# Row and edge jobs moved into the counting stage, and x and node numbers side by side in one gathered table, in a graph kernel on one Trainium2 core

## What is computed

```python
h = relu(edge_attr @ W1.T + b1); w = h @ W2.T + b2          # edge jobs
agg = segment_sum(w * x[src], dst, N)
x = layernorm(x + relu(x @ Ws.T + bs + agg @ Wn.T + bn))    # row jobs where agg = 0
# then: 10 passes of out = 0.9 * spmm(out) + 0.1 * h, a layernorm,
# 16 passes of h = 0.9 * A_norm(h) + 0.1 * x, a layernorm,
# two graph convolutions with PReLU, a layernorm
```

## Time and profile before

| | us |
|---|---|
| median of 3 runs | 12,517.22 (12,501.07 to 12,523.01) |
| the profiled execution | 12,463.33 |
| its span in the profile | 12,461.6 |
| busy in the span: PE, DVE, ACT, POOL | 4,407; 4,689; 3,793; 7,373 |
| first 2,681 us: all that stands ahead of the passes | 21.5% of the span |
| granted TensorE clock, mean | 0.548 of full |

### The profile page before, as it was taken

One profiled execution on the slowest core, in us unless ns is written; L12 is line 12 of the kernel. 1 busy time (PEld: TensorE's weight loads), 2 busy tenths in 40 slices (PEclk: granted clock), 3 DMA queues, 4 the chain that ended last, 5 costly groups with the idle time before them and its releaser, 6 DMA issues. The chain is left out here.

```text
span 12461.6 us, 88179 instructions
## 1 busy us (share of the span) xinstructions
PE 4407.2 (35%) x18774; PEld 3275.0 (26%) x18774; DVE 4688.8 (38%) x11607; ACT 3793.3 (30%) x11417; POOL 7372.8 (59%) x7464
## 2 busy tenths in 40 slices
PE   4610462343333333332033333333334332212533
PEld 3300352332222222221022222222222221111422
DVE  7900232233333333355034444444444443233333
ACT  3400462243222222226342222222223231134322
POOL 6767105426666667665656666666666666654455
PEclk8655555555555555555555555555555555555555
DMA  3211221133333333333123333333333333221211
GB/s 51 56 26 20 67 83 44 38 71 88 85 88 88 85 88 90 87 84 104 34 79 87 88 89 88 88 93 94 95 94 98 95 96 82 73 57 54 63 35 31
DMA packets 791320, 919.85 MB, mean 74 GB/s; under 512 B 258979, under 2 KB 676541, under 8 KB 790749
## 3 DMA queue, kind: packets, MB, share of 16 engines
q1 hardware_dynamic: 558638, 591.29, 15.5%
q0 software_dynamic: 232064, 323.36, 13.4%
q10 hardware_dynamic: 144, 0.10, 0.0%
HBM read 533.07 MB, written 388.06 MB: 74 GB/s over the span
## 5 line engine op out<-in xcount | busy, mean ns | idle before, releaser
L1624 POOL DMA_INDIRECT l_g<-tab,l x4704 | 4620.1, 982 | 2536.7 <-issue 1355.4
L1824 DVE TENSOR_TENSOR_SCAN l_w<-l_m,l_w,bank 96x512 f32<-96x512 bf16 x1248 | 1590.3, 1274 | 4350.1 <-remote 2797.1
L1661 PE MATMUL bank<-ident,l_w 96*128 96x96 f32 x5096 | 1092.0, 364 | 2537.9 <-DVE l_w L1824 2176.1
L1724 ACT ACTIVATE l_o<-l_o,coef_d 128x96 f32<-128x96 f32 x2940 | 857.1, 363 | 3162.2 <-DVE l_o L1852 1813.6
L1650 PE MATMUL bank<-ident,l_g 128*96 128x128 f32 x5096 | 1267.5, 399 | 1345.3 <-DMA l_g<-tab,l 602.5
L1661 PEld LDWEIGHTS bank<-ident,l_w 96*128 96x128 f32 x5096 | 846.5, 222 | 2833.4 <-DVE l_w L1824 2368.4
L1650 PEld LDWEIGHTS bank<-ident,l_g 128*96 128x96 f32 x5096 | 913.4, 190 | 1725.1 <-DMA l_g<-tab,l 640.4
L1720 ACT ACTIVATE l_o<-bank,coef_s 128x96 f32<-128x96 f32 x1764 | 450.4, 345 | 1809.7 <-remote 970.6
L278 PE MATMUL bank<-tail_up,v 96*96 96x500 f32 (+1 forms) x298 | 296.4, 1098 | 925.7 <-issue 660.4
L993 POOL DMA_INDIRECT XS<-in_x_dram,dst_i x196 | 198.0, 1010 | 710.7 <-DVEq L1337 647.3
L315 PE MATMUL bank<-ident,tail_up 96*125 96x96 f32 (+1 forms) x596 | 159.5, 423 | 867.8 <-issue 476.2
(11 more groups left out here) (292 smaller groups left out, 10764.1 us busy)
## 6 DMA issues: line engine op xcount, KB each, us to landing
tab<-l_o SPq DMA_DIRECT2D x1176, 192.0 KB
l_g<-tab,l POOLq DMA_INDIRECT x4704
l_m<-mask_d SPq DMA_DIRECT2D x784, 96.0 KB
l_m<-mask_s SPq DMA_DIRECT2D x490, 96.0 KB
x3t<-XS SPq DMA_DIRECT2D x98, 192.0 KB
prep_x<-in_x_dram SPq DMA_DIRECT2D x100, 187.5 KB
x1t<-prep_a SPq DMA_DIRECT2D x100, 187.5 KB
x3d<-prep_b SPq DMA_DIRECT2D x100, 187.5 KB
```

The source lines that it names most:

```text
L1624: nc.gpsimd.indirect_dma_start(out=tile(G[q % RG], t), out_offset=None, in_=tables[0:table_at + (2 - p % 2) * TR, :] if p else first, in_o ...
L1661: last = nc.tensor.transpose(b_bank(q)[:, u * D:(u + 1) * D], W[q % RW][:, u:GE:U], self.ident[0:D, 0:D])
L1724: last = a.activation(tile(O[q % RO], t), tile(O[q % RO], t), ACT.Copy, scale=self.coef_d[:, t:t + 1])
L1824: v.tensor_tensor_scan(out=W[q % RW][:, :], data0=masks[q % RM][:, :], data1=a_bank(q)[0:D, :], initial=W[(q - 1) % RW][:, GE - 1:GE] if q ...
```

## The change

Row jobs and edge jobs leave `prepare` and run inside `count_edges`, which is now written out for every engine: iteration k does tiles 2k and 2k+1, row job k (its steps spread over the following four iterations) and every other time an edge job. Row and edge jobs get one PSUM bank for each step (4 to 7) instead of two; x buffers are 8 instead of 5, result buffers 4 instead of 3; they, the count tables and the edge attributes lie in a new tile XM [128, 196 x 104]. XS is no longer allocated this early. SP also copies x into a new table `x_meta` of 104 floats a node, in 25 pieces, between its other transfers.

In `prepare`, SP copies `meta` beside x in that table. POOL gathers `meta` by source, waits for the copy, and gathers x and `meta` together by destination: two rounds instead of three. Edge records are made in two halves: the first (groups 0 to 24) ahead of the sums loop as soon as its rows have landed, the second ahead of the loop's group 12 (FIRST); the scatter waits for each half by itself. In the sums loop one semaphore ("stepped") stands for several, and its steps lag by one more turn. The core of the diff:

```diff
+HALF, FIRST = 25, 12
+        self.both_t = self.dram("x_meta", [N, D + MF])
+            self.XM = tmp("XM", [P, NT * (D + MF)])
...
             @block.sync
+                for k in range(LAST):
+                    n = k // 2
+                    if k % 2 == 0 and n < NI - 1:
+                        if n:
+                            sp.wait_ge(nears, n * U)
+                        load(n + 1)
+                    if k + 3 < JN:
+                        load_x(k + 3)
+                    if k % 4 == 1 and k // 4 < JOIN:
+                        some = slice(k // 4 * (N // JOIN), (k // 4 + 1) * (N // JOIN))
+                        sp.dma_start(self.both_t[some, 0:D], i["x"][some, :]).then_inc(R["joined"], 16)
+                    if 0 <= k - 5 < JN:
+                        store_rows(k - 5)
...
             @block.vector
+                for k in range(LAST):
+                    for t in (2 * k, 2 * k + 1):
+                        if t < NT:
+                            pairs(t)
+                            if t + 1 < NT:
+                                digits(t + 1)
+                        if 0 <= t - 2 < NT:
+                            tiles_before(t - 2)
+                        if t % U == 2 and t // U + 1 < NI:
+                            high_digits(t // U + 1)
+                        if t % 2 == 0:
+                            if 0 <= k - 2 < JN:
+                                rows(k - 2)
+                        else:
+                            if 0 <= k - 3 < JN:
+                                scale_rows(k - 3)
+                            if k % 2 and 0 <= (k - 3) // 2 < NI:
+                                gate((k - 3) // 2)
...
             @block.tensor
+                    for t in (2 * k, 2 * k + 1):
+                        if t < NT:
+                            count(t)
+                        if 0 <= t - 1 < NT:
+                            lookup(t - 1)
+                        if t % U == 0 and 0 <= n - 1 < NI:
+                            weigh(n - 1)
+                        if t % U == 1 and n < NI:
+                            if n == 0:
+                                pe.wait_ge(R["ea"], 32)
+                            turn_edges(n)
+                        if t % U == 3 and n < NI:
+                            hide(n)
+                        if t % 2 == 0:
+                            if k < JN:
+                                turn_rows(k)
+                        elif 0 <= k - 1 < JN:
+                            mult_rows(k - 1)
...
             @block.scalar
+                    for t in (2 * k, 2 * k + 1):
+                        if t < NT:
+                            snapshot(t)
+                        if t % U == 0 and 0 <= n - 1 < NI:
+                            rectify(n - 1)
+                        if t % U == 2 and n < NI:
+                            copy_edges(n)
+                        if t % 2 == 0:
+                            if 0 <= k - 4 < JN:
+                                normal_rows(k - 4, 0)
+                        else:
+                            if k < JN:
+                                lift_rows(k)
+                            if 0 <= k - 2 < JN:
+                                root_rows(k - 2)
+                            if 0 <= k - 4 < JN:
+                                normal_rows(k - 4, 1)
...
     def prepare(self):
+                for k, (index, of, into) in enumerate(((self.src_i, self.meta, ms), (self.dst_i, self.both_t, rows_in))):
+                    if k:
+                        pool.wait_ge(S["joined"], 16)
+                    for g in range(NGP):
+                        q = k * NGP + g
                         if q >= RG:
                             pool.wait_ge(self.fills(q), self.full(q - RG))
...
                 for g in range(NGP):
-                    q = 3 * NGP + g
+                    q = 2 * NGP + g
+                    if g in (0, HALF):
+                        pool.wait_ge(S["made"], 1 + g // HALF)
...
             @block.sync
+                    sp.dma_start(self.both_t[:, D:D + MF], self.meta[0:N, :]).then_inc(S["joined"], 16)
...
             @block.vector
+                for g in range(NGP + 3):
+                    if g in (0, FIRST):
+                        part = g // FIRST
+                        landed = NGP + (NGP if part else HALF)
+                        for q in range(landed - RG, landed):
+                            dve.wait_ge(self.fills(q), self.full(q))
+                        self.edge_records(dve, link, halves[part], part, ms, md, work[part], record, row, S)
+                        dve.sem_inc(S["made"], 1)
                     if g < NGP:
                         scan(g)
```

More of the change, by code:

```diff
@@ new lines, in _ @@
+                load(0)
+                for n in range(3):
+                    load_x(n)
+                sp.wait_ge(R["blank"], 1)
+                with nc.allow_non_contiguous_dma(reason="the attributes of four edges of each partition"):
+                    sp.dma_start(ea[:, 0:GF * U * ED].rearrange("p (g c) -> p g c", c=U * ED),
+                                 i["ea"][0:GF * GE, :].rearrange("(g p u) c -> p g (u c)", p=P, u=U)
+                                 ).then_inc(R["ea"], 16)
+                    sp.dma_start(ea[0:REST // U, GF * U * ED:NT * ED],
+                                 i["ea"][GF * GE:E, :].rearrange("(p u) c -> p (u c)", u=U)).then_inc(R["ea"], 16)
@@ new lines, in turn_edges, with hide, weigh @@
+                    last.then_inc(G["turned"], 1)
+                def hide(n):
+                    pe.wait_ge(G["copied"], n + 1)
+                    nc.tensor.matmul(edge_in[0:D, :], self.w1[:, :], eat[:, :], start=True, stop=True
+                                     ).then_inc(G["hidden"], 1)
+                def weigh(n):
+                    pe.wait_ge(G["rect"], n + 1)
+                    if n:
+                        pe.wait_ge(G["gated"], n)
+                    for u in range(U):
+                        last = nc.tensor.matmul(edge_out[:, u * D:(u + 1) * D], hid[:, u * P:(u + 1) * P], self.w2[:, :],
+                                                start=True, stop=True)
+                    last.then_inc(G["product"], 1)
@@ L808, in lookup @@
-                def lookup(t, u, b):
-                    pe.wait_ge(split.sem, split.at + t + 1)
-                    if not (isinstance(t, int) and t < 2):
-                        pe.wait_ge(fars.sem, fars.at + t - 1)
-                    k = 0
-                    for c in range(2):
-                        for part in (coarse, fine):
-                            last = nc.tensor.matmul(look[u % 2], oht[:, b, c, u * P:(u + 1) * P],
-                                                    part[u % 2][:, c * LO:(c + 1) * LO], start=k == 0, stop=k == 3)
-                            k += 1
-                    last.then_inc(looked.sem, 1)
@@ L835, in _ @@
-                steps(pe, body)
+                pe.wait_ge(R["ones"], 3)
+                for k in range(LAST):
+                    n = k // 2
+                    for t in (2 * k, 2 * k + 1):
[16 more added lines that the diff above has]
+                            mult_rows(k - 1)
@@ L854, in _, with snapshot @@
-                steps(act, body)
+                a_ = nc.scalar
+                def snapshot(t):
+                    if t:
+                        act.wait_ge(product, t)
+                    if t >= 2:
+                        act.wait_ge(split, t - 1)
+                    a_.activation(snap[t % 2][:, :], hist[0], ACT.Copy).then_inc(snapped, 1)
+                    act.wait_ge(snapped, t + 1)
+                    if t >= 2:
+                        act.wait_ge(looked, t - 1)
+                    a_.activation(coarse[t % 2][:, :], snap[t % 2][:, :], ACT.Copy).then_inc(rounded, 1)
@@ L1337, in _ @@
-                dve.sem_inc(S["made"], 1)
-                for g in range(NGP + 2):
+                for g in range(NGP + 3):
+                    if g in (0, FIRST):
+                        part = g // FIRST
+                        landed = NGP + (NGP if part else HALF)
[3 more added lines that the diff above has]
+                        dve.sem_inc(S["made"], 1)
@@ L1340, in _, with edge_records @@
                     if g < NGP:
                         scan(g)
+                    if 0 <= g - 3 < NGP:
+                        scale_sums(g - 3)
                     if 0 <= g - 2 < NGP:
-                        scale_sums(g - 2)
-                    if 0 <= g - 1 < NGP:
-                        sums(g - 1)
-        self.groups += 4 * NGP
-    def edge_records(self, dve, link, ms, md, work, record, row, S):
+                        sums(g - 2)
+        self.groups += 3 * NGP
+    def edge_records(self, dve, link, h, part, ms, md, work, record, row, S):
```

677 lines of the change are left out of this document (296 added, 381 removed).

## The result

The changed kernel takes **11,793.3 us** (median of 4, 11,777.9 to 11,810.0) against 12,514.3 us (median of 4): ratio **0.9425**, 95% interval 0.9408 to 0.9442, 721 us faster. I had forecast 12,132 us, 385 faster. The direction was right, the size was not: the time lies 177 us under the range. The profiled execution has a span of 11,781.9 us against 12,461.6.

A forecast was written before the change was run, and what follows sets the result against it. No single engine bounds the part ahead of the passes, a row of non-overlapping stages. Its sums end at 2,236 instead of 2,620.7 us, gaining 385: 12,078, or 12,132 us on the median's scale; range 11,970 to 12,410.

The forecast's parts named there:

- Cost of an iteration of counting: Counting with row and edge jobs: 10.4 us per two tiles, between 8.3 and 12.6; stage 1,060 us instead of 549.
- Rival A: Counting overlaps almost wholly: 8.8 us per iteration, 900 us for the stage, 11,972 us in all; chance 0.13.
- B: Overlap in counting fails: 12.6 us per iteration plus 40 us for copies, 1,320 us, 12,392 in all; chance 0.15.
- Marks after counting: Stages after counting: round one ends at 1,412 us, round two 1,672, sums 2,236, passes' first gather near 2,300.
- Copy of meta on the path: Copy of meta into x_meta ahead of round two: at most 187 us, under round one's 246, so 0 added.
- C: Copy of meta isn't covered: POOL stands up to 150 us ahead of round two, 12,282 us; chance 0.10.
- Stop in the scatter: POOL waits in the scatter for the second half of edge records, from 1,806 to 1,887 us.
- A round and the 647 us stop: Ahead of the scatter: one round of 196 gathers and POOL's 647.3 us stop for the row jobs are removed.
- D: PE crawls within written-out counting: 15.3 us per iteration, 490 us more, 12,622 us, slower by 0.8%; chance 0.07.
- crawl: PE beside dense gathers starts a step only each 1.4 or 2.8 us; row jobs take 49.5 us, not 6.96.
- E: Edge records' wait returns at the sums' 12th group: 384 us instead of 61, 12,455 us in all; chance 0.03.
- The passes the same within 20 us: Passes, unchanged in code and order: their length stays the same within 20 us.

The follow-up runs named there:

- The short subtraction: Kernel before, and changed kernel, with GpSimd's subtraction in counting cut to 8 of 512 columns: 10,090 us and 10,125 us.
- free: Sets of runs in which the kernel before took 10,299, 10,327 and 10,311 us.
- hampered: Sets of runs in which the kernel before took 12,453 and 12,489 us, as well as the first measurement (12,514.3 us).
- before again: Kernel before, unchanged, run again for its own trace in a hampered set: 12,450 us.
- before, paced: Kernel before, with GpSimd's gathers in three rounds waiting for the row jobs: 12,045 us hampered (ratio 0.9642), 10,407 us free.
- changed kernel again: Changed kernel, unaltered, timed again: 11,777.6 us hampered (ratio 0.9432), 10,177.7 us free (ratio 0.9848).
- whole records: Changed kernel with edge records made in one piece after the whole second round instead of in halves: 11,738 us, hampered set.

## Why the forecast was wrong, step by step

- **Cost of an iteration of counting** ("The lower bound is 8.3 ... I take the middle, 10.4", 1,060 us): this is the step that failed. Measured 7.10 us, under what I had called a lower bound. Between the profiled executions the gain was 680 us, 295 over the forecast: 322 from the end of counting and 21 from the stages after it, less 49 for the passes. The medians add 41, since the profiled execution lay further under its median before the change than after it. Both halves of the sum were too high: the bound, 8.3 against 6.6 us of the busiest engine, and the slack on top, 2.1 against 0.5 us. The middle between full overlap and none had no row behind it, and the overlap is nearly full. As for the bound, two of the rates that I added up are not constants. PE's share (8.3) came from stretches at granted clocks of 0.68 and 0.51; in the shared stage it was 0.80, and the same row-job multiply took 316 ns instead of 410. Busy: 594.97 / 100 = 5.9 us. I had the row with the clock and corrected only upwards, to 9.1 (its rows give 9.4: 3.42 x 0.68 / 0.51 + 4.87). The run with more multiplies shows the clock rising with PE's load, and the same instruction getting shorter. Lines of row jobs, of the kernel before (1376 to 1947 us) and of the changed one (73 to 813 us):

```profile
L1065 PE MATMUL bank<-wa,prep_xt 98*125 98x96 f32 x657 | 151.4, 410 | 0.0
```

```profile
L907 PE MATMUL bank<-wa,XM 98*125 98x96 f32 x800 | 130.4, 316 | 2.1 <-DVEq L801 2.1
```

  VectorE's share (8.1) held 2.77 us a tile, of which much was waiting for GpSimd; measured 6.6. The short subtraction shows how large that part is: 2.67 down to 1.58 us a tile in the kernel before, and some 1.0 us per two tiles in the changed one. That they meet less often with a tile each 3.6 us instead of 2.8 is my reading of it. What holds the stage 0.5 us above its busiest engine was not isolated. Rival A (8.8 per iteration) was the nearest and still too dear; B was far off.
- **ScalarE**, 6.9 forecast, 6.4 measured, was 88% busy, second to VectorE with 91%, part of which is waiting for GpSimd; PE, which I had put first, was at 82%.
- **Marks after counting**, from GpSimd's first gather of round one to the first pass: about 1,134 us forecast, 1,109 measured. Round one 246, measured 245. Round two 260, measured 276. Copy of meta on the path 0: right, no stop; C fell. First half's numbers landed 381 us in, records begun at 386. Stop in the scatter 81, measured 74.5. Sums' last store 1,070 us in, measured 1,047 (1,890.9). Each within 25 us, though in part by errors that cancel: three sum groups passed ahead of the stop instead of 5.8 (68 us apart, 62 forecast), four beside the second half as forecast, and the last 35 at 4.9 us each instead of 5.6. In a free set the scatter has no stop.
- **A round and the 647 us stop are gone**: right, though for less general a reason than I gave. The table is worth 245.7 us, measured alone. The stop was long only because PE was hampered; free, it is 112.7.
- **D, a crawl within counting**: false; counting is alike in both kinds of sets. Its price rested on a misread line: the 2,797 us of the earlier trace rows are put down to "remote", an unknown releaser, not to PE. **E**: false.
- **The passes the same within 20 us**: wrong, they took 49 longer. Hampered traces scatter by as much: 8,722 (before again) and 8,775 (before, paced) against 8,762 (changed kernel again) and 8,719 (whole records). In free sets, where they scatter less, the changed kernel took 7,641 us and its variants 7,619 to 7,634, the variants of the kernel before 7,607 to 7,615. So some 10 to 35 us may belong to the change; nothing shows why.

The gain in the start of the first pass can be put together from the runs. *Free* (before taken from the kernel with more multiplies, 1,825.9): 174 us = 246 for the table + 112 for the stop - 183 for the longer counting, with 1 us of rest. (Counting was 547 us in that trace; with the 524 of the same set the gain would be near 150.) Taking the jobs from beside the gathers and putting them into counting, without the table, is a loss of some 70 us there (1,897.2 against 1,825.9). *Hampered*: 717 us (2,668.2 to 1,951.0, the two kernels run again), of which pacing alone, with all jobs left in place, gives 433 (2,668.2 to 2,235.5). From there the changed kernel gains 284.5 more. One round less is worth 245.7 of that if it costs the same as in a free set; this split isn't shown. The whole kernel says it without such sums: 712 us hampered against 150 free, so some 560 us of the gain exist only where PE crawls, and pacing alone brings 445. So most of the size came from ending a crawl, and the placing of the jobs in counting was one way of that.

What stays open: what hampers PE. In the stretches it shows "issue" and starts in step with GpSimd's gathers, and no run changed how PE gets its instructions. PE may not be the only engine hit. In the passes of the changed kernel the waits of VectorE and ScalarE are partly put down to "issue" and "remote" where the set is hampered, and to named engines where it is free. First the hampered trace, then the free one (total us, times, longest):

```profile
DVE l_w L1836 <- remote: 2770.2, 310, 31.1
...
ACT l_o L1736 <- issue: 1553.0, 331, 31.4
...
DVE l_w L1836 <- issue: 1004.6, 238, 33.8
```

```profile
DVE l_w L1836 <- PE bank L1662: 4011.4, 1177, 262.2
...
ACT l_o L1736 <- DVE l_o L1864: 2640.4, 705, 48.0
```

The gathers run longer too: in round two a median of 1,095 ns against 947. Whether these engines are held themselves or only wait for PE, the traces don't say. That a set of runs is hampered or free as a whole was seen, not explained.

## What to carry to other kernels

An engine's busy time read at one load is not a floor at another: before adding shares of two stages, look at the granted clock in each, and at which of its instructions run longer beside another engine's. Filling an already busy stage is cheaper than the sum of its engines' times suggests; here 689 us of jobs cost 163. Take the range of unchanged code from several traces before calling a difference of 20 us nothing or something. And where an engine sits idle for "issue" beside steady gathers, first see whether another set of runs shows it, and try pacing the gathers before moving the work.

## Not expected of the hardware

- Back-to-back indirect gathers (1.25 us each) slow TensorE sevenfold in some sets of runs (183 multiplies in 490 us) and not at all in others (1,309), with the same code; the whole kernel before then takes 12,453 to 12,514 or 10,299 to 10,327 us. One gather per 1.8 us in bursts of a few, or one per 3.6 us, did no such harm in a hampered set.
- TensorE's granted clock in one stage went from 0.63 to 0.88 with 75% more multiplies, and the same multiply from 398 to 310 ns; it went to 0.95 where VectorE held PE back less and the same multiplies came in 59% of the time.
- VectorE lost 213 of 524 us to GpSimd's 512-column subtraction, nearly as long as the subtractions themselves take (196 x 1.16 = 227).
